# Four batches of attention as one ordered stream, with each batch's later chain placed between the next batch's units

## What is computed

```
q = w8a8_linear(layernorm(x), wq, bq)              # rows rounded to 8 bits by their largest magnitude
k, v = cond @ wk.T + bk, cond @ wv.T + bv          # 16 heads of 32 columns, 512 keys
scores = q @ k.T / sqrt(32) + mask                 # 512 x 512 for each head and batch
o = softmax(scores) @ v
x = x + tanh(g_xattn[1]) * w8a8_linear(o, wo, bo)  # the rows of o rounded by their largest magnitude
h = silu(bitlinear(layernorm(x), W1))              # 512 -> 2048, rows rounded again
x = x + tanh(g_ffn[1]) * bitlinear(h, W2)          # 2048 -> 512, the hidden rows rounded again
```

## Time and profile before

| engine | busy us | share of the span | instructions |
|---|---|---|---|
| TensorE matmuls (PE) | 935.4 | 84% | 5912 |
| TensorE weight loads (PEld) | 637.5 | 57% | 5912 |
| VectorE (DVE) | 752.4 | 67% | 1934 |
| ScalarE (ACT) | 572.6 | 51% | 1120 |
| GpSimd (POOL) | 90.4 | 8% | 73 |

### The profile page before, as it was taken

One profiled execution on the slowest core, in us unless ns is written; L12 is line 12 of the kernel. 1 busy time (PEld: TensorE's weight loads), 2 busy tenths in 40 slices (PEclk: granted clock), 3 DMA queues, 4 the chain that ended last, 5 costly groups with the idle time before them and its releaser, 6 DMA issues.

```text
span 1118.9 us, 16360 instructions
## 1 busy us (share of the span) xinstructions
PE 935.4 (84%) x5912; PEld 637.5 (57%) x5912; DVE 752.4 (67%) x1934; ACT 572.6 (51%) x1120; POOL 90.4 (8%) x73
## 2 busy tenths in 40 slices
PE   3999799999999869998599659996599965999657
PEld 2777577777677547776456325563255632556324
DVE  6888852625341366777499666996669966699664
ACT  3454231212221257777389336893368933689334
POOL 4444100000000001112000100001000010000100
PEclk9998999999999989999799869998699986999869
DMA  6340400202011186687996501465014650100000
GB/s 220 116 132 3 151 1 1 76 1 76 1 45 69 61 304 255 239 325 223 324 208 150 151 0 39 115 151 151 0 39 115 151 151 0 39 1 2 1 0 38
DMA packets 54529, 115.37 MB, mean 103 GB/s; under 512 B 6832, under 2 KB 6832, under 8 KB 53424
## 3 DMA queue, kind: packets, MB, share of 16 engines
q1 hardware_dynamic: 45648, 88.62, 27.5%
q0 software_dynamic: 6016, 25.17, 5.7%
q10 hardware_dynamic: 2784, 0.54, 0.2%
HBM read 84.95 MB, written 29.36 MB: 102 GB/s over the span
## 4 chain that ended last, share of the span: by engine, by line
PE 41%; DVE 11%; ACT 5%; issue 4%; POOL 2%; DMA 2%; POOLq 0%; SPq 0%; DVEq 0%; ACTq 0%
PE psum L1404 8%; PE psum L1421 6%; PE psum L1445 6%; PE psum L1376 6%; PE psum L1475 5%; ACT qxT L1117 2%; POOL xres L966 2%; PE psum L1254 2%; PE psum L1256 1%; PE psum L1255 1%; DVE xn L1686 1%; PE psum L1461 1%; PE psum L1430 1%; PE psum L1293 1%; DMA k<-k_dram 1%
## 5 line engine op out<-in xcount | busy, mean ns | idle before, releaser
L1697 DVE CUSTOM_DVE_ANT_0 psum<-psum,m_in 128x512 f32<-128x512 f32 x256 | 174.6, 701 | 12.2 <-issue 9.3
L1191 ACT ACTIVATE probs<-psum,neg_max 128x512 f32<-128x512 f32 x256 | 174.5, 689 | 11.9 <-DVE neg_max L1697 11.6
L1404 PE MATMUL psum<-ident,probs 128*128 128x128 f32 x1024 | 154.7, 274 | 0.0
L1376 PE MATMUL psum<-k,q 128*128 128x512 f32 x256 | 125.3, 495 | 17.9 <-ACT probs L1191 9.2
L1404 PEld LDWEIGHTS psum<-ident,probs 128*128 128x128 f32 x1024 | 127.6, 141 | 21.2 <-issue 3.8
L505 PE MATMUL psum<-w_sb,hT 128*128 128x512 f32 x256 | 115.0, 592 | 0.0
L389 ACT ACTIVATE hT<-psum,b_col 128x256 f32<-128x256 f32 x64 | 26.9, 471 | 134.6 <-PE psum L425 134.6
L1724 DVE COPY probsT<-psum 128x512 f32<-128x512 f32 x128 | 87.8, 686 | 2.5 <-PE psum L1404 2.3
L1421 PE MATMUL psum<-probsT,vv 128*32 128x256 f32 x1024 | 80.1, 389 | 8.9 <-DVE probsT L1724 3.5
L1182 ACT COPY probsT<-psum 128x512 f32<-128x512 f32 x128 | 74.9, 585 | 22.1 <-PE psum L1404 19.5
L423 PE MATMUL psum<-xselT_hi,w_hi 128*128 128x256 f32 x256 | 82.2, 321 | 4.2 <-ACT onehotT L383 4.2
(11 more groups left out here) (220 smaller groups left out, 1898.3 us busy)
## 6 DMA issues: line engine op xcount, KB each, us to landing
q<-q_dram SPq DMA_DIRECT2D x64, 256.0 KB, 7.8
k<-k_dram SPq DMA_DIRECT2D x64, 256.0 KB, 5.4
c_in<-in_ctx_dram SPq DMA_DIRECT2D x8, 1024.0 KB, 5.5
bw_in<-in_L_ffn_W_dram SPq DMA_DIRECT2D x8, 1024.0 KB, 8.6
xres<-in_x_dram SPq DMA_DIRECT2D x4, 1024.0 KB, 5.1
w_raw<-in_L_ffn_w_dram POOLq DMA_DIRECT2D x4, 1024.0 KB, 5.2
w_sb<-in_L_ffn_w_dram SPq DMA_DIRECT2D x1, 4096.0 KB, 13.5
x_mid_dram<-xres SPq DMA_DIRECT2D x4, 1024.0 KB, 4.5
```

What stands on the lines that cost most here:

```text
L1191: act.activation(probs[:, u % 4, :], psum[u % SCORE_BANKS][:, :], ACT.Exp, scale=-1.0, bias=neg_max[:, u:u + 1], accum_out=prob_sum[:, nt, ...
L1376: pe.matmul(psum[u % SCORE_BANKS][:, :], q4[:, h, nt * P:(nt + 1) * P], k4[:, h, :], start=True, stop=True).then_inc(score_psum, 1)
L1404: mm = pe.transpose(turn_bank(u)[:, l * P:(l + 1) * P], probs[:, u % 4, l * P:(l + 1) * P], ident[:, :])
L1697: dve.tensor_tensor_reduce(bank[:, :], bank[:, :], m_in[:, nt, :], -1.0, LOWEST, ALU.add, ALU.min, neg_max[:, u:u + 1]).then_inc(masked_re ...
```

## The change

The loops of the four batches become one loop over steps `s` on each engine. Step `s` issues the parts of the attention for one unit out of `NU` = 256 and then, from the second batch on, one numbered step `j` of the chain of the batch before: `b, j = divmod(s - SIDE_FIRST, UNITS)` with `SIDE_FIRST` = 12. The whole feed-forward layer of the batch before is issued at one step, `BURST` = 26, that is behind unit 38 of each batch. For the fourth batch no units are left and its chain runs alone.

PSUM is divided anew: banks 0 to 2 scores (as before), **banks 3 and 4 turns**, bank 5 AV, **banks 6 and 7 everything of the chain and of the feed-forward layer**, in one fixed order by turns. The back-turn O of a half group no longer lies beside its AV result: it takes a slot in the ring of turn banks (`o_turn`, `unit_turn`), and it is read by VectorE one step later (`O_SCALE`), behind that step's mask and copy. In the diff below, both functions are TensorE's up to `side(b, j)`; `side(b, j, link)` is VectorE's.

```diff
-        LAG = 3
-        SCORE_BANKS, TURN_BANKS = 3, 3
+        SCORE_BANKS = 3
+        LAG = 3
+        NU = B * UNITS
+        AV_FIRST = LAG + UH
+        AV_STEPS = (1, 2, 4, 5)
+        AV_COPY, O_TURN, O_SCALE = AV_FIRST + 6, AV_FIRST + 7, AV_FIRST + 8
+        SIDE_FIRST = O_SCALE + 1 - UH
+        BURST = 26
+        STEPS = NU + SIDE_FIRST + BURST + 1
+        def unit_turn(u):
+            return u + max(0, u // UH - 1)
+        def o_turn(n):
+            return min(UH * (n + 2), NU) + n
+        def turn_bank(n):
+            return psum[SCORE_BANKS + n % 2]
...
+                def attend(s):
...
+                        n = unit_turn(u)
+                        pe.wait_ge(probs_ready, u + 1)
+                        if n >= 2:
+                            turn_wait(pe, n - 2)
+                        for l in range(T):
+                            mm = pe.transpose(turn_bank(n)[:, l * P:(l + 1) * P], probs[:, u % 4, l * P:(l + 1) * P], ident[:, :])
...
+                    hg = half_group(s, O_TURN)
+                    if hg is not None:
+                        n = o_turn(hg)
+                        pe.wait_ge(av_ready, hg + 1)
+                        turn_wait(pe, n - 2)
...
+                def side(b, j):
+                    if j == 4:
+                        pe.wait_ge(oq_ready, b * T + T)
+                        side_rows(b, "rows", 0)
+                        side_rows(b, "rows", 1)
+                    if 6 <= j < 6 + T:
+                        project_out(b, j - 6)
+                    if j == 24:
+                        pe.wait_ge(xq_ready, b * T + T)
+                        side_rows(b, "rows2", 0)
+                        side_rows(b, "rows2", 1)
+                    if j == BURST:
+                        up(b, 0)
+                        up(b, 1)
+                        turn_hidden(b, 0)
+                        up(b, 2)
+                        turn_hidden(b, 1)
+                        up(b, 3)
+                        down(b, 0)
+                        turn_hidden(b, 2)
+                        down(b, 1)
+                        turn_hidden(b, 3)
+                        down(b, 2)
+                        down(b, 3)
...
+                def side(b, j, link):
+                    if j == 2:
+                        attention_scales(b, link)
+                        rounded_attention(b)
+                    if 7 <= j < 7 + T:
+                        scaled_out(b, j - 7)
+                    if 9 <= j < 9 + T:
+                        residual_stats(b, j - 9, link)
+                    if 13 <= j < 15 + NEWTON_STEPS:
+                        residual_root(j - 13, link)
+                    if j in (19, 20):
+                        dve.wait_ge(xn_ready, b * T + 2 * (j - 18))
+                        largest(link, amax, xn, range(2 * (j - 19), 2 * (j - 19) + 2))
+                    if j == 21:
+                        row_scales(b, link)
+                        rounded_rows(b)
```

```diff
+                def attend(s, link):
...
+                        dve.tensor_tensor_reduce(bank[:, :], bank[:, :], m_in[:, nt, :], -1.0, LOWEST, ALU.add, ALU.min,
+                                                 neg_max[:, s % UNITS:s % UNITS + 1]).then_inc(masked_ready, 1)
...
+                        dve.tensor_copy(probsT[:, (hg + 1) % 2, r, :, (nt % 2) * P:(nt % 2) * P + P],
+                                        turn_bank(n)[:, :].rearrange("p (l n) -> p l n", l=T)).then_inc(turn_copied[n % 2], 1)
...
+                    n = half_group(s, O_SCALE)
+                    if n is not None:
...
+                        dve.tensor_tensor(
+                            o_rows[:, n0:n0 + 2, g * P:(g + 1) * P].rearrange("p t (r d) -> p t r d", r=HPG),
+                            turn_bank(m)[:, 0:HALF].rearrange("p (t r d) -> p t r d", t=2, r=HPG),
...
+                            ALU.mult).then_inc(turn_copied[m % 2], 1)
```

More of the change, by code:

```diff
@@ new lines, in turn_wait, with half_group @@
+        def turn_wait(eng, n):
+            eng.wait_ge(turn_copied[n % 2], n // 2 + 1)
+        AV_BANK = psum[5]
+        def half_group(s, delay):
+            n, i = divmod(s - delay, UH)
+            return n if 0 <= n < B * HG and i == 0 else None
+        SIDE = {}
+        for block in ([("rows", i) for i in range(2)] + [("out", t) for t in range(T)] + [("rows2", i) for i in range(2)]
+                      + [("up", t, f) for t in range(2) for f in range(FQ)] + [("turn", 0, i) for i in range(2)]
+                      + [("up", 2, f) for f in range(FQ)] + [("turn", 1, i) for i in range(2)]
+                      + [("up", 3, f) for f in range(FQ)] + [("down", 0)] + [("turn", 2, i) for i in range(2)]
+                      + [("down", 1)] + [("turn", 3, i) for i in range(2)] + [("down", 2), ("down", 3)]):
+            SIDE[block] = len(SIDE)
@@ L1019, in _ @@
                 sp.wait_ge(v_saved[2], 16)
-                sp.dma_start(m_in[:, :, :], rows(mask, 0)).then_inc(m_loaded, 16)
+                load_mask(0, 0)
+                load_mask(0, 1)
                 sp.wait_ge(qxT_psum, 8)
-                sp.dma_start(vv[:, :, :], rows(v_dram, 0)).then_inc(vv_loaded, 16)
+                sp.wait_ge(v_saved[0], 16)
+                for g in range(GROUPS):
+                    load_values(0, g)
                 sp.wait_ge(k_saved[0], 32)
@@ L1245, in _ @@
                     project(b)
-                for b in range(B):
-                    batch(b)
+                for s in range(STEPS):
+                    attend(s)
+                    b, j = divmod(s - SIDE_FIRST, UNITS)
+                    if b >= 1:
+                        side(b - 1, j)
             @block.tensor
@@ new lines, in project_out @@
+                def project_out(b, t):
+                    n = side_number(b, "out", t)
+                    if t == 0:
+                        for i in range(2):
+                            side_read(pe, side_number(b, "rows", i))
+                    side_free(n)
+                    for c in range(CT_):
+                        mm = pe.matmul(psum[side_bank(n)][:, :], qxT[:, c, t * P:(t + 1) * P], woT[:, c, :],
+                                       start=(c == 0), stop=(c == CT_ - 1))
+                    mm.then_inc(side_psum, 1)
@@ L1474, in down @@
+                def down(b, t):
+                    n = side_number(b, "down", t)
+                    for i in range(2):
+                        side_read(pe, side_number(b, "turn", t, i))
+                    side_free(n)
+                    hold(psum[side_bank(n)])
                     for f in range(FT):
-                        mm = pe.matmul(psum[6 + t % 2][:, :], hqT[:, t % 2, f, :], bw2T[:, f, :],
+                        mm = pe.matmul(psum[side_bank(n)][:, :], hqT[:, t % 2, f, :], bw2T[:, f, :],
@@ L1534, in _ @@
                 pe.wait_ge(v_ready, B * T)
-                first_scores(0)
-                for b in range(B):
-                    batch(b)
+                for s in range(STEPS):
+                    attend(s)
+                    b, j = divmod(s - SIDE_FIRST, UNITS)
+                    if b >= 1:
+                        side(b - 1, j)
             @block.vector
```

764 lines of the change are left out of this document (373 added, 391 removed).

## The result

The changed kernel took 1137.36 us (median of 4 runs, 1136.05 to 1144.13) where the kernel before took 1119.05 in the same comparison: a ratio of 1.0172, 95% interval 1.0144 to 1.0200. It is slower by 1.7%; 1132 was forecast. The span of the profiled execution grew from 1118.9 to 1136.4 us, though the mean granted clock rose from 0.937 to 0.951 and PE's share of the span is still 84%. Three of the four executions of the changed kernel took 1136.05 to 1138.11 us at a mean clock of 0.951 or 0.952; the fourth, at 0.942, took 1144.13.

The account below looks back on a forecast made before the run. Attention was taken to run at TensorE's pace. A period stays near 139.9 us (84.0 + 17 + 38 + 0.8 = 139.8); the first batch's +8 and the end's -0.7 and +4.6 give +12, so 1132 us, range 1120 to 1146 (0.62).

Parts of the forecast that it names:

- Step 1: Between batches: three of the four later chains no longer stand alone, 37.4 us from last score to first `up`, drain included.
- Step 2: Attention: with two turn banks and O in their ring, half a group takes 10.5 us instead of 8.8.
- Turn 1 behind the scaling: Turn ring: turn 1 waits until VectorE's scaling, behind mask and copy, has read O; 1.25 us per half group.
- O behind the copy: Turn ring: O waits for VectorE's copy of turn 6; 0.5 us per half group.
- For the other slots there is room: Turn ring: odd turns' ScalarE copies are done after 1.34 us, the turn two slots on comes after at least 1.4.
- Step 3: Chain work between attention units: adds 17 us a batch, bounds 10 and 33.
- the restart: Attention behind the feed-forward layer: the exponential's table load is hidden under three waiting turns but for 0.8 us.
- Step 4: Feed-forward layer issued whole at j=26: 38 us, bounds 33.4 and 43, where it took 36.0.
- The fourth layer: Fourth batch's feed-forward layer at the end: narrow banks and a slow-clock start, 39.6 us against 35.0, +4.6.
- the late mask: Rival: the second mask half lands after its first use, each join pays a few us; no separate chance given.
- The ring does not bite: Rival, attention: pace stays at 1.10 us a unit, 1095 us in all; chance 0.23 including only half biting.
- The lumps add up: Rival, chain between units: 25 us instead of 17 and clock falls in the holes, 1165 us; chance 0.15.

Follow-up runs that it names:

- experiment 4: Changed kernel with the chain's steps 4 to 26 issued as one piece at step 26, ahead of the feed-forward layer: 1166.97 us, ratio 1.0414.
- experiment 1: Changed kernel with VectorE's scaling of a half group's result moved ahead of that step's mask and copy: 1110.27 us, ratio 0.9918.
- experiment 2: Changed kernel with VectorE's scaling ahead of mask and copy, and O out of the turn ring, beside the AV result in bank 5: 1096.47 us, ratio 0.9784.
- Experiment 3: Kernel before with two turn banks in place of three, O still beside the AV result: 1122.64 us, ratio 1.0018.
- experiment 9: Kernel before with SyncE's load of the first batch's input rows issued behind that batch's keys and queries: 1132.13 us, ratio 1.0100.
- experiment 7: Changed kernel with the rounding of the third hidden tile back on ScalarE, as in the kernel before: 1141.78 us, ratio 1.0205.

## Why the prediction was right, and where it was off

**Step 1, the joins go.** Right: no drain and no chain stands alone at the three joins, and experiment 4 puts a figure on the chain between the units, 10 us saved in each batch.

**Step 2, the narrow ring.** Right, and the deciding one. 10.5 us was forecast (its terms, 8.8, 1.25 and 0.5, add to 10.55), 10.74 came. Turn 1 behind the scaling: priced 1.25, 1.22 by experiment 1. O behind the copy: priced 0.5; O starts 0.98 us behind turn 7 (619.05 to 620.03) and 0.44 where it need not wait (experiment 2), so 0.54. What I had not priced is turn 0 behind ScalarE's copy of turn 7: I had counted the copy from turn 7's start (1.34) without the exponential that stands ahead of it in ScalarE's queue. The copy ended 1.58 after turn 7 began (619.05 to 620.63), and unhindered turn 0 would have started at 1.48; with the hand-over (0.11 from the copy's end to turn 0's weight load at 620.74) and the lost head start of that load (0.03 ahead of the turn where it is 0.21 without a wait) it started at 1.72, which makes 0.24. "For the other slots there is room" was the error, 1.9 us a period. The three add to 2.00, and 1.95 was measured. Experiment 3 adds what the text left open: in the old order two banks by themselves cost the half group nothing.

**Step 3, the chain.** 17.8 with the restart, measured 20.0. The order of the pieces was right (normed rows, maxima and rounding in series are the dearest), the hole in front of the turn was 2.95 us, but a fall of the clock was not in the term: two stretches of 6.7 us ran at 0.50, worth up to 4.6 us (my estimate). PE was busy 2.35 us of the 5.9 before the second drop and 2.93 of the 4.8 before the first; that the idle time brought the drops was not isolated. How much of the 2.2 us between 17.8 and 20.0 is the clock was not isolated. The restart's 0.8 us did not show: the exponential's table load (730.00 us, 1.28 long) ran while TensorE was in the `down` blocks, and the first turn came 0.42 us after its score.

**Step 4, the lump.** 37.4 measured, 38 forecast. That the lump runs at the full clock behind busy units was assumed in the base of 32.1 (2.9 us of it against before's 0.92), and no run had shown it; measured, the clock was 1.00 from 699 to 737 us. The waits for banks that PE's list names (for ScalarE's copies of the hidden rows, VectorE's residual add and the Silu: 5.0, 3.5 and 1.6 us over four lumps) are 2.5 us in a lump, where I had 4.6; the wait behind the Silu's table load is 1.17, where I had 1.28; some 1.6 us over my base of 32.1 has no name there. (The upper bound of 43 was mis-added: 33.4 and eight times 1.1 is 42.2.) The fourth layer took 37.9 us, not 39.6.

**Missed: the first score.** -3.8 us between the two profiles. I read the diff of SyncE's loads for the late mask only and not for what stood ahead of the first keys, though the 8.75 us wait was in the trace. Without this gain the sum would have been 21, not 17.5, so two errors of opposite sign made 1132 look closer than its working was: that was luck. How much of it belongs to the change is open: the move of the load alone shortens the wait by 1.3 to 2.9 us, and the moment at which TensorE comes to that wait differs by more from one profile to another (536.7 to 542.0 us).

**The rivals.** "The ring does not bite" fell with the 10.74; its 1095 is what experiment 2 reached (1096.5). "The lumps add up" asked for 25 us and got 20; it named the clock in the holes rightly (0.50 from 672.8 to 679.5 and from 689.9 to 696.6 us). The late mask did not occur: in VectorE's list of waits no transfer of the mask appears.

## What to carry to other kernels

In this kernel the ring of banks was as slow as its latest reader (a half group of 10.74 us, and 9.52 with that reader's scaling put first): before a slot is given to a new user, count when that user's reader gets its turn in its own queue, and put the short read (the scaling, 0.41 us) ahead of the long ones (mask and copy, 0.70 and 0.69). Two small edits (the order of one instruction and a slot taken out) were worth 41 us; with them the rearrangement is 23 us below the kernel before, without them 18 above. Before a load is moved back, look at who else waits in the queue of its first consumer: in experiment 9, VectorE's stood still for 14.70 us; in the changed kernel, in GpSimd's, no mask waited longer than 4.9.

## What the runs showed of the hardware that I had not expected

TensorE's clock fell to half inside the stream of the attention, though none of its waits there was longer than 3.0 us: at 672.8 us, after 4.8 us with PE busy 2.93, and at 689.8, after 5.9 us with PE busy 2.35; each time it ran at 0.50 for some 6.7 us, and the work in between was slow (a turn 1.09 for 0.63). In experiment 7 it fell inside a wait of 1.04 us (0.50 from 644.7 us on), in a place where the changed kernel's profile kept it. A turn that waited also had no weight load running ahead of it. Timeline of the changed kernel, weight loads (PEld) and matmuls, behind a score without and with a wait:

```profile
615.28 0.57 PEld L1482 LDWEIGHTS psum<-ident,probs 128*128 128x128 f32 x4
615.49 0.60 PE L1482 MATMUL psum<-ident,probs 128*128 128x128 f32 x4
...
622.64 0.42 PEld L1482 LDWEIGHTS psum<-ident,probs 128*128 128x128 f32 x4 [1.33 <-ACT probs L1272]
622.67 0.63 PE L1482 MATMUL psum<-ident,probs 128*128 128x128 f32 x4 [1.05 <-DVE o_rows L1807]
```

In the seven turns without a wait from 611 to 625 us of the changed kernel the loads start 0.21 us ahead of the matmuls; in the three whose loads had waited (by 1.32, 0.39 and 1.33 us; loads at 611.88, 620.74 and 622.64) both start 0.03 apart. And each AV block with a score behind it, from 866 to 872 us of before and from 612 to 624 of the changed kernel, is followed by 0.41 us in which no weights are loaded ("issue"): 0.57 from block to score, where from a turn without a block to the score it is 0.35 to 0.38.
